# A macaron block on one Trainium2 core: the sums of exp(q) for every second chunk as pairwise additions on GpSimd, and new orders on all engines

## The reference

```python
x = x + 0.5 * ffn(layernorm(x))
x = x + attn(layernorm(x))
x = x + 0.5 * ffn(layernorm(x))

# ffn: lt = 16 tokens from token 1; m1, m2 are products of even and odd ones, per batch
h = gelu(x @ W1.T + scale * (x @ m1.T) + b1, exact)
out = h @ W2.T + scale * (h @ m2.T) + b2

# attn: 16 heads of 8, no softmax over keys
q, k, v = heads(x @ Wq.T + bq), heads(x @ Wk.T + bk), heads(x @ Wv.T + bv)
f(t) = exp(t/sqrt(8) @ R - 0.5 * sum((t/sqrt(8))**2))
kv = sum_n f(k)[n, :] v[n, :]
z = 1 / (sum_d f(q)[n, d] + 1e-8)
out = (z * (f(q) @ kv)) @ Wo.T + bo
```

## Time and profile before

| | us |
|---|---|
| median of 3 runs | 168.94 |
| the three runs | 169.96, 168.44, 168.94 |
| the profiled execution, own time | 168.41 |
| its span (first to last instruction) | 166.7 |
| busy: PE, DVE, ACT, POOL | 156.5, 125.6, 124.1, 91.3 |

### The profile page before, as it was taken

One profiled execution on the slowest core, in us unless ns is written; L12 is line 12 of the kernel. 1 busy time (PEld: TensorE's weight loads), 2 busy tenths in 40 slices (PEclk: granted clock), 3 DMA queues, 4 the chain that ended last, 5 costly groups with the idle time before them and its releaser, 6 DMA issues.

```text
span 166.7 us, 3400 instructions
## 1 busy us (share of the span) xinstructions
PE 156.5 (94%) x1036; PEld 139.1 (83%) x1036; DVE 125.6 (75%) x418; ACT 124.1 (74%) x249; POOL 91.3 (55%) x126
## 2 busy tenths in 40 slices
PE   6868999999999999899999998699999999999994
PEld 6835998999899889588898976588999989989993
DVE  1799895999489627999999999999997952582112
ACT  3399997687797999467999768899978564774330
POOL 5646648018999979968986892036513299000000
PEclk9999999999999999999999999999999999999999
DMA  4990445371213343322133124434346253255204
GB/s 101 325 292 16 128 129 189 127 193 64 64 65 110 83 148 107 122 67 65 42 110 104 67 65 126 159 95 130 139 117 203 91 152 97 95 152 167 63 0 126
DMA packets 31425, 19.55 MB, mean 117 GB/s; under 512 B 2624, under 2 KB 28464, under 8 KB 31408
## 3 DMA queue, kind: packets, MB, share of 16 engines
q1 hardware_dynamic: 30976, 19.27, 38.6%
q10 hardware_dynamic: 432, 0.07, 0.2%
HBM read 11.94 MB, written 7.40 MB: 116 GB/s over the span
## 4 chain that ended last, share of the span: by engine, by line
PE 83%; ACT 6%; DVE 4%; DMA 2%; issue 2%; SPq 1%; DVEq 0%; ACTq 0%
PE quad L811 33%; PE quad L792 9%; PE quad L793 8%; PE quad L794 8%; PE ps_g L846 4%; PE quad L828 4%; PE ps_t L865 4%; PE quad L830 3%; PE quad L829 3%; DMA X<-in_x_dram 2%; ACT xn L488 2%; PE ps_r L835 2%; ACT gl L528 1%; DVE ex L713 1%; ACT xn L493 1%
## 5 line engine op out<-in xcount | busy, mean ns | idle before, releaser
L811 PEld LDWEIGHTS quad<-w2e,gl 128*128 128x128 f32 x496 | 60.3, 192 | 2.7
L811 PE MATMUL quad<-w2e,gl 128*128 128x128 f32 x496 | 60.6, 275 | 0.0
L528 ACT ACTIVATE gl<-quad,cols 128x512 f32<-128x512 f32 x64 | 42.9, 685 | 15.2 <-PE quad L794 14.9
L792 PE MATMUL quad<-xh,w1h 128*128 128x512 f32 x64 | 28.6, 447 | 2.2 <-DVE xl L631 1.5
L488 ACT ACTIVATE xn<-X,nmr,rstd 128x128 f32<-128x128 f32 x61 | 25.1, 487 | 2.4 <-DVE nmr L603 2.4
L793 PE MATMUL quad<-xl,w1h 128*128 128x512 f32 x64 | 25.3, 395 | 0.0
L794 PE MATMUL quad<-xh,w1l 128*128 128x512 f32 x64 | 25.2, 394 | 0.0
L699 DVE TENSOR_TENSOR X<-quad,X 128x512 f32<-128x512 f32 (+1 forms) x16 | 10.6, 671 | 17.2 <-PE quad L811 16.0
L440 POOL TENSOR_TENSOR X<-X,b2h 128x512 f32<-128x512 f32 x16 | 21.5, 1368 | 0.2 <-DVE X L732 0.2
L413 POOL TENSOR_SCALAR veps<-mv 128x4 f32<-128x4 f32 (+1 forms) x16 | 4.8, 302 | 26.4 <-DVE mv L131 26.4
L415 POOL TENSOR_TENSOR rstd<-veps,mhalf 128x4 f32<-128x4 f32 (+1 forms) x16 | 16.4, 1027 | 1.3
(11 more groups left out here) (109 smaller groups left out, 280.7 us busy)
## 6 DMA issues: line engine op xcount, KB each, us to landing
ev<-token_rows SPq DMA_DIRECT2D x7, 512.0 KB, 3.8
folded<-tq SPq DMA_DIRECT2D x12, 256.0 KB, 2.0
land<-folded SPq DMA_DIRECT2D x48, 64.0 KB, 2.0
folded<-atq SPq DMA_DIRECT2D x8, 256.0 KB, 2.0
aland<-folded SPq DMA_DIRECT2D x32, 64.0 KB, 2.0
X<-in_x_dram SPq DMA_DIRECT2D x7, 256.0 KB, 6.5
out_dram<-X SPq DMA_DIRECT2D x7, 256.0 KB, 2.7
w1t<-in_w1t_dram SPq DMA_DIRECT2D x1, 256.0 KB, 3.5
```

Of the source, the lines that this page charges most:

```text
L528: act.activation(gl[:, f % 2, j], ps_h[j % 2], ACT.Gelu, bias=cols[:, j:j + 1]).then_inc(s_gelu, 1)
L792: pe.matmul(ps_h[j % 2], w1h[:, w, blk], xh[:, f % XT], start=True, stop=False)
L811: ins = pe.matmul(y[:, n * P:(n + 1) * P], gl[:, f % 2, j, n * P:(n + 1) * P], w2e[:, f // PER_B % 2, j], start=(j == 0), stop=(j == HB - 1))
```

## The change

For chunks 1, 3, 5 and 7 (`BY_PAIRS`) the stage `z_sums` is now GpSimd's: three additions, of the first and last four exponents of each head (256 results per partition), of the pairs of these (128), and of the last two (64), each behind the one before. The intermediate results lie in `wb`. The two waits on k_war and k_wv stand before the first. VectorE keeps chunks 0, 2, 4 and 6. All engines have a new order. Of the orders the diff below keeps the lines that the text speaks of.

```diff
+BY_PAIRS = (1, 3, 5, 7)
...
     "sp": (
...
-        "rows.4 put.9 put.10 land.9 land.10 rows.5 put.11 put.12 land.11 land.12 rows.6 put.13 down.8.3 put.14 "
...
+        "aland.1 aland.2 aput.4 aput.5 aland.3 aland.4 aland.5 aput.6 aland.6 aput.7 aland.7 put.8 land.8 rows.4 "
+        "rows.5 put.9 put.10 land.9 land.10 put.11 put.12 land.11 land.12 rows.6 put.13 put.14 land.13 land.14 "
...
     "pool": (
-        "stats.0 rest.0 stats.1 stats.2 stats.3 stats.4 stats.5 stats.6 stats.7 bias.0 bias.1 bias.2 astats.0 bias.3 "
-        "astats.1 bias.4 bias.5 bias.6 astats.2 abias.0 abias.1 astats.3 abias.2 abias.3 aturn.0 astats.4 astats.5 "
-        "aturn.1 bias.7 abias.4 abias.5 abias.6 aturn.2 astats.6 z_eps.0 aturn.3 z.0 z_eps.1 astats.7 aturn.4 z.1 "
-        "z_eps.2 abias.7 z.2 bias.8 aturn.5 stats.8 z_eps.3 z.3 aturn.6 stats.9 z_eps.4 bias.9 z.4 z_eps.5 aturn.7 "
-        "stats.10 z.5 stats.11 z_eps.6 stats.12 z.6 z_eps.7 z.7 stats.13 stats.14 stats.15 bias.10 bias.11 bias.12 "
...
+        "stats.0 rest.0 stats.1 stats.2 bias.0 bias.1 stats.3 stats.4 stats.5 stats.6 stats.7 abias.0 bias.2 bias.3 "
+        "astats.0 astats.1 bias.4 bias.5 aturn.0 astats.2 abias.1 abias.2 astats.3 astats.4 astats.5 bias.6 bias.7 "
+        "abias.3 aturn.1 astats.6 abias.4 abias.5 aturn.2 aturn.3 z_eps.0 abias.6 z.0 z_sums.1 z_eps.1 astats.7 "
+        "aturn.4 z.1 aturn.5 z_eps.2 stats.8 z.2 z_sums.3 aturn.6 z_eps.3 stats.9 z.3 aturn.7 z_eps.4 stats.10 "
+        "z_sums.5 z_eps.5 z.4 z.5 bias.8 bias.9 stats.11 z_eps.6 z_sums.7 stats.12 z_eps.7 z.6 stats.13 z.7 bias.10 "
+        "abias.7 stats.14 stats.15 bias.11 bias.12 bias.13 bias.14 bias.15 "
...
     "act": (
-        "norm.0 rest.0 first_w1h.0 first_w1h.1 first_w1h.2 turn.0 norm.1 load.0 first_w1h.3 up.0.0 turn.1 up.0.1 "
-        "norm.2 up.0.2 up.0.3 turn.2 norm.3 up.1.0 up.1.1 norm.4 up.1.2 up.1.3 w1h.1 norm.5 norm.6 up.2.0 turn.3 "
...
-        "anorm.6 feat.3.1 qturn.0 mix.0.1 anorm.7 exp.3.0 exp.3.1 aturn.5 feat.4.0 qturn.1 feat.4.1 gram.3 qturn.2 "
...
-        "turn.8 exp.6.0 gram.5 feat.7.0 norm.9 mix.2.1 qturn.4 norm.10 feat.7.1 w1h.4 exp.6.1 qturn.5 exp.7.0 exp.7.1 "
...
+        "norm.0 rest.0 first_w1h.0 first_w1h.1 turn.0 norm.1 first_w1h.2 first_w1h.3 up.0.0 turn.1 up.0.1 load.0 "
+        "up.0.2 up.0.3 norm.2 up.1.0 up.1.1 turn.2 norm.3 up.1.2 up.1.3 norm.4 norm.5 w1h.1 turn.3 norm.6 up.2.0 "
...
+        "norm.9 turn.8 norm.10 gram.5 feat.7.0 feat.7.1 qturn.3 exp.6.0 exp.6.1 w1h.4 mix.2.1 qturn.4 qturn.5 exp.7.0 "
+        "exp.7.1 up.8.0 up.8.1 turn.9 gram.7 up.8.2 up.8.3 up.9.0 up.9.1 turn.10 norm.11 up.9.2 up.9.3 norm.12 "
...
     "dve": (
...
-        "stats.2 first_w1l.0 norm.1 first_w1l.1 moments.2 turn.0 first_w1.3 stats.3 stats.4 norm.2 first_w1l.2 "
-        "stats.5 first_w1l.3 moments.3 moments.4 turn.1 stats.6 w2.0 norm.3 norm.4 moments.5 odd.1 turn.2 moments.6 "
...
-        "down.6.3 head_sums.0.0 ablocks.4 feat.0.0 astats.6 down.7.3 ablocks.5 amoments.6 astats.7 head_sums.0.1 "
-        "feat.0.1 head_sums.1.0 feat.1.0 z_sums.0 amoments.7 head_sums.1.1 feat.1.1 z.0 head_sums.2.0 z_sums.1 "
-        "feat.2.0 head_sums.2.1 feat.2.1 z.1 mix.0.0 z_sums.2 head_sums.3.0 feat.3.0 ablocks.6 head_sums.3.1 z.2 "
...
-        "z_sums.5 stats.10 head_sums.6.0 moments.10 feat.6.0 head_sums.6.1 o.3 feat.6.1 norm.9 turn.8 mix.2.0 "
-        "head_sums.7.0 odd.4 z.5 norm.10 feat.7.0 blocks.9 w1.4 blocks.10 stats.11 head_sums.7.1 w1l.4 feat.7.1 "
-        "moments.11 o.4 z_sums.6 stats.12 w2.4 turn.9 norm.11 moments.12 o.5 z.6 z_sums.7 stats.13 odd.5 mix.3.0 "
...
+        "stats.2 first_w1l.0 norm.1 moments.2 turn.0 first_w1.3 stats.3 first_w1l.1 norm.2 b2h.0 first_w1l.2 "
+        "first_w1l.3 moments.3 stats.4 turn.1 w2.0 moments.4 stats.5 stats.6 moments.5 moments.6 norm.3 stats.7 "
...
+        "down.6.3 astats.6 ablocks.4 ablocks.5 amoments.6 head_sums.0.0 feat.0.0 down.7.3 astats.7 head_sums.0.1 "
+        "feat.0.1 head_sums.1.0 feat.1.0 amoments.7 z_sums.0 head_sums.1.1 feat.1.1 z.0 head_sums.2.0 feat.2.0 "
+        "ablocks.6 head_sums.2.1 feat.2.1 z.1 head_sums.3.0 mix.0.0 feat.3.0 z_sums.2 head_sums.3.1 feat.3.1 o.0 "
...
+        "head_sums.6.0 head_sums.6.1 feat.6.0 z.4 norm.10 feat.6.1 odd.4 turn.8 blocks.9 blocks.10 head_sums.7.0 "
+        "mix.2.0 w1.4 z.5 head_sums.7.1 o.3 w1l.4 feat.7.0 feat.7.1 o.4 stats.11 z_sums.6 moments.11 stats.12 o.5 "
+        "turn.9 moments.12 norm.11 mix.3.0 z.6 w2.4 stats.13 odd.5 norm.12 moments.13 blocks.11 w1.5 blocks.12 z.7 "
...
     "pe": (
-        "lead.0 select.0 select.1 turn.0 up.0.0 turn.1 up.0.1 up.0.2 up.0.3 turn.2 up.1.0 up.1.1 down.0.0 down.0.1 "
-        "down.0.2 up.1.2 up.1.3 turn.3 down.0.3 down.1.0 down.1.1 down.1.2 up.2.0 up.2.1 split_weights.0 up.2.2 "
...
-        "mix.1.1 qturn.3 qk.6.0 o.2 qk.6.1 qk.6.2 qk.6.3 gram.5 o.3 qk.7.0 qk.7.1 mix.2.0 mix.2.1 qturn.4 qk.7.2 "
-        "qk.7.3 o.4 qturn.5 gram.6 up.8.0 up.8.1 o.5 gram.7 up.8.2 up.8.3 mix.3.0 up.9.0 up.9.1 down.8.0 down.8.1 "
...
+        "lead.0 select.0 turn.0 select.1 up.0.0 turn.1 up.0.1 up.0.2 up.0.3 up.1.0 up.1.1 down.0.0 turn.2 up.1.2 "
+        "down.0.1 up.1.3 down.0.2 down.0.3 down.1.0 down.1.1 turn.3 down.1.2 split_weights.0 up.2.0 up.2.1 down.1.3 "
...
+        "mix.1.1 o.2 qk.6.0 qk.6.1 qk.6.2 qk.6.3 gram.4 gram.5 qk.7.0 qk.7.1 qk.7.2 qk.7.3 mix.2.0 qturn.3 mix.2.1 "
+        "o.3 qturn.4 gram.6 qturn.5 o.4 up.8.0 up.8.1 o.5 gram.7 up.8.2 up.8.3 mix.3.0 up.9.0 up.9.1 mix.3.1 up.9.2 "
...
@@ -198,6 +198,9 @@
         vd = sb("vd", [P, 3])
         vs = sb("vs", [P, 3])
         wb = sb("wb", [P, 3, D])
+
+        z4 = wb[:, 0:2].rearrange("p k (m h d) -> p (k m) h d", m=2, h=HEADS)
+        z2 = wb[:, 2].rearrange("p (n h d) -> p n h d", n=NT, h=HEADS)
         wv2 = sb("wv2", [P, D])
         wah = sb("wah", [P, TOK], F32R)
         wal = sb("wal", [P, TOK], F32R)
@@ -264,6 +267,7 @@
             sem(f"s_{n}") for n in ("zs", "ze", "zr", "qn", "qt", "qte", "g", "o", "x2")]
 
         m_gs, m_kv, m_kvm, m_mp, m_mo = [sem(f"m_{n}") for n in ("gs", "kv", "kvm", "mp", "mo")]
+        s_pairs = sem("s_pairs")
         s_out = sem("s_out")
 
         folded = nc.dram_tensor("folded", (FC + CHUNKS, P, TOK), F32, kind="Internal").ap()
@@ -448,6 +452,20 @@
                     pool.wait_ge(a_hi, i + 1)
                     pool.tensor_tensor(as_tiles(xal[:, i % AH]), in_order(aland[:, i % ALAND]),
                                        as_tiles(xah[:, i % AH].bitcast(F32)), ALU.subtract).then_inc(a_lo, 1)
+                if stage == "z sums":
+                    mine = heads(qk[:, i % 2, :, 0, :])
+                    k = 2 * BY_PAIRS.index(i)
+                    pool.wait_ge(s_exp, 2 * i + 2)
+                    wait(pool, s_ze, i)
+                    if k == 0:
+                        pool.wait_ge(k_war, 1)
+                        pool.wait_ge(k_wv, 1)
+                    pool.tensor_tensor(z4, mine[:, :, :, 0:4], mine[:, :, :, 4:8], ALU.add).then_inc(s_pairs, 1)
+                    pool.wait_ge(s_pairs, k + 1)
+                    pool.tensor_tensor(z2, z4[:, :, :, 0:2], z4[:, :, :, 2:4], ALU.add).then_inc(s_pairs, 1)
+                    pool.wait_ge(s_pairs, k + 2)
+                    pool.tensor_tensor(zs[:, 0].rearrange("p (n h) -> p n h", n=NT), z2[:, :, :, 0], z2[:, :, :, 1],
+                                       ALU.add).then_inc(s_zs, 1)
                 if stage == "z eps":
                     pool.wait_ge(s_zs, i + 1)
                     wait(pool, s_zr, i)
```

## The result

The changed kernel takes 167.22 us (median of 4 runs, 166.9 to 167.42) against 169.43 for the kernel before (4 runs, 168.44 to 169.96): ratio 0.989, 95% interval 0.985 to 0.993. A later comparison gave 166.63 (6 runs) against 169.34 (10 runs), 0.982 with 0.978 to 0.987. So it is 1 to 2% faster. The kernel before scatters more than the changed one (168.28 to 170.71 over its 10 runs of the later comparison, against 166.25 to 167.1), and its profiled execution, 168.41, is one of its faster ones. Executions in a slower state of the chip are left out of every median here. The profiled execution of the changed kernel took 167.42 for a span of 165.7, 1.0 less than before, of 2.75 us forecast.

What follows compares the result with a forecast made beforehand. VectorE's queue was taken to set when up.8.0 starts, with TensorE dense behind it. Terms 2.25 + 0.8 - 0.3 = 2.75 us saved gave a median of 166.2; own range 164.9 to 167.6, with A and B 164.9 to 168.7.

Steps and rivals of the forecast that it cites:

- The attention stage, 2.25: VectorE's queue up to up.8.0 gets shorter: 2.55 - 0.5 + 0.2 = 2.25 us gained, ends 0 and 3.7.
- the 2.55: Work leaving VectorE's queue ahead of up.8.0: three z sums (1.77) and stats.11 (0.78), 2.55 us less.
- 0.5 for VectorE idle at its o.3 near 102: VectorE reaches o.3 at 101.7, TensorE's o.3 is done at 102.2, so VectorE stands idle for 0.5 us.
- The 1.77: Three of four z reductions taken off VectorE stand ahead of up.8.0, at 0.59 each: 1.77 us.
- The z chain, 1.6: GpSimd's three additions per odd chunk take 0.65, 0.43, 0.33 and waits, 1.6 us; the longer latency is covered.
- The start, 0.8: In the first 17 us, putting ScalarE's w2t scaling and norm.2 behind gelus gains 0.8 us, ends -0.3 and 1.2.
- The clash, 0.3: GpSimd's new additions exclude VectorE instructions with two SBUF inputs near w1.4 and w1l.4: 0.3 us lost.
- Behind up.8.0, nothing: TensorE stays full from up.8.0 to the end, so a microsecond saved before it is saved at the end.
- A (gaps only move): New order's kvm, qt and o.3 in a row eat the attention gain of 2.25: 168.4 us, chance 0.17.
- B: Rival: each of four pair chains on GpSimd holds up a VectorE instruction on the path, 2 us: 167.9, chance 0.1.
- C: Rival: TensorE's o.3 comes late behind qturn.3 and the slower z, ending at 107.9: 170.7 us, chance 0.08.
- D: Rival: all gaps closed, 3.7 in the attention stage plus 0.8 at the start: 164.4 us, chance 0.03.

Runs made afterwards that it cites:

- the one-word edit: The changed kernel with VectorE's feat.6.0 moved ahead of head_sums.6.1: 166.43 us, ratio 0.985 to the kernel before.
- the one sum of chunk 3: The changed kernel with chunk 3's z sum back on VectorE, behind head_sums.4.1: 167.17 us, ratio 0.991 to the kernel before.
- the queue cleared: Old orders, four sums on GpSimd, with bias.8 and bias.9 ahead of z.5 and abias.7 behind z_eps.6: 171.37 us, ratio 1.011 to the kernel before.
- the sums alone: The kernel before, in its old orders, with the z sums of chunks 1, 3, 5, 7 on GpSimd: 172.16 us, ratio 1.021.
- the one with the biases: Old orders, four sums on GpSimd, with abias.7, bias.8 and bias.9 moved behind z.5: 174.87 us, ratio 1.035 to the kernel before.

## Why the prediction was right or wrong

**The whole.** Forecast 166.2 with 164.9 to 168.7; measured 167.22 in the first comparison and 166.63 in the second. Direction and range held. Against the median before of the same comparison the gain is 2.2 and 2.7, of 2.75 forecast; the profiled span gained 1.0 and 1.7. That the 2.7 comes so near is in part luck: the forecast was made from one of the faster executions before, and the medians before lie 1.0 above it. By the lowest times the gain is 1.5 and 2.0. The parts held less well than the sum.

**The attention stage, 2.25: 1.67 and 1.73.** The stage did get shorter by what left VectorE's list, but this step is too large by 0.55, and what fills the 2.55 up again is not what I named. I put 0.5 for VectorE idle at its o.3 near 102; it did not wait:

```profile
104.32 0.68 DVE L750 TENSOR_TENSOR X<-ps_t,X 128x512 f32<-128x512 f32 x1
104.91 0.68 DVE L692 TENSOR_TENSOR w1l<-w1r,w1h 128x512 fp32r<-128x512 f32 x1
```

It came to o.3 at 104.32, not at 101.7, and TensorE's mix.2.0 at 101.52, not 99.7. (0.3 of each difference is the later first `up`.) The lateness began upstream, in TensorE's gaps: o.2 behind mo (0.8), then qk.7.0 behind feat.6.0 (0.5), the second of which the one-word edit shows (0.35 of the stage). I had added VectorE's queue as a sum of starts without its own waits and put only one new wait against it, 0.5; the changed kernel has two others, 0.51 and 0.45, for ScalarE. I had also put the wait of 1.4 down to VectorE, since "the exp itself comes behind VectorE's subtraction"; it was ScalarE's list that kept that exp for 5.3 us. up.8.0 was forecast at 105.8 less the start's gain and came at 106.69 and 106.09, short of the 107.5 that would have refuted it. Another sign of being wrong did come, a small one: TensorE's o.3 waits for qt (ScalarE is done with it at 102.98, o.3 starts at 103.07).

**What the sums do and what the orders do.** I forecast them as one. The runs part them: -0.59 and +2.74 alone, -1.67 together. The 1.77 that I booked for the sums is 0.6 in the stage (0.3 for the one sum of chunk 3), and the orders, for which my terms leave 0.78 - 0.5 + 0.2 = 0.5, are worth 1.1 where od doesn't meet qn (0.59 + 0.5). So the reason that I gave first carries a third of the gain. "Cover, then, until GpSimd runs over 2 us late" holds with the new orders, where VectorE's z never waits. With the old ones VectorE waited for z (1.33, and still 0.86 with the queue cleared) and TensorE for xal, which I had not priced at all.

**The z chain, 1.6: 1.57.** Its terms were 0.65, 0.43, 0.33 and are 0.73, 0.40, 0.29. That its length is hidden was right as well, with the new orders: with one addition in place of three B1 was 0.05 shorter.

**The start, 0.8: nothing.** At down.0.0 the forecast holds: it starts at 16.37 for 17.19 of the earlier trace rows, and first up to down.0.0 took 5.64 for 6.78, 1.1 less, of which 0.44 is turn.2:

```profile
14.89 0.47 PE L810 MATMUL quad<-xh,w1h 128*128 128x512 f32 x1 [0.16 <-ACT gl L546]
...
16.37 1.05 PE L829 MATMUL quad<-w2e,gl 128*128 128x128 f32 x8
```

But up.3.0 starts at 29.98 for 29.86, waiting for a gelu, which is only 0.2 ahead of before when counted from the first `up`, and A is 57.40 for 57.39. The step that failed is "a microsecond saved" at the start "is one saved at the end": ScalarE has the deferred load and norms still to do, and TensorE meets it again. With the start of before, A is 0.33 longer (57.73), above all nine with the new start, so the new start gives at least 0.3 and the rest of the new order of the first FFN takes it back.

**The clash, 0.3: none on the path here.** I took the additions for the danger and wrote that the moved biases cover the rest. Both halves were wrong. In the changed kernel GpSimd pays, being second:

```profile
99.67 1.52 POOL L477 TENSOR_TENSOR qn<-qk,zr 128x512 f32<-128x512 f32 x1
...
104.97 3.01 POOL L444 TENSOR_TENSOR X<-X,b2h 128x512 f32<-128x512 f32 x2
```

(1.08 and 2.55 undisturbed.) qn stands beside the xl of 99.57, the biases beside the w1l of 104.91, and nobody waits for either. The biases would be the costly ones: two of them on w1.4 cost 0.7 of the stage, and the three on all four of its instructions 2.5 (B2 of 11.78 for 9.29). "A clash costs 0.5" was read from one row; a single one cost 0.9 to 1.1 here (od 1.07 for 0.16, one w1 1.35 for 0.34, nmr 1.25 for 0.15), nearly the whole GpSimd instruction, whatever the size of VectorE's own.

**Behind up.8.0, nothing: +0.33 and +0.20.** C is longer by that. One gap of 0.25 is seen, ahead of up.9.0 (the last product before it starts at 111.35, it at 111.83). TensorE was not quite full from up.8.0 on, where I had it full. GpSimd's chain of chunk 7 took longer there (1.00 for its first addition at 111.26, beside w2.4), with nobody waiting. The rest of the 0.33 is not settled.

**The rivals.** A (gaps only move) is part of the truth: 0.5 of the stage and the start. B is real as a mechanism and not on the path in the changed kernel. C did not come: TensorE's o.3 ended at 104.2, 3.7 ahead of its point. D is out; some 2 us of gaps remain.

## What to carry to other kernels

Work moved to a less loaded engine is paid for in that engine's queue: before pricing its length, ask what stands behind it and who waits for that, and move the reorder with it. Look for small VectorE instructions with two inputs in SBUF that start within a long GpSimd addition, since each can cost nearly that whole addition; a word's place in the list can be worth more than the work's size. Work taken off a full engine gives back only what its next wait leaves: before booking it, look for the input that the engine will now be too early for. A lead won at the start counts only once it is still there at the stage that bounds the kernel; compare stretches between landmarks, not spans.

## What the runs showed of the hardware

A VectorE instruction of 8 columns took 1.07 and 1.08 where it takes 0.16, and one of 4 columns 1.25 for 0.15, each started 0.02 to 0.06 behind a GpSimd product or addition of 1.08, 1.09 or 1.29 us. Behind one of 0.73 the one of 4 columns took 0.69. In these runs the price follows the other engine's instruction.

TensorE's granted clock fell in two kernels, each time behind waits. With the sums alone it is 0.66 in 110:115, after 3.55 us of work in the 5 us ahead (rows above), and in the one with the biases 0.66 too, after 1.75:

```profile
105.00:110.00 5.00, 1.75 (x14) 1.36 (x12) 5.00 (x6) 2.44 (x7) 4.16 (x4) 1.00 0.14 52
110.00:115.00 5.00, 4.14 (x15) 3.53 (x16) 5.00 (x19) 4.01 (x7) 1.63 (x3) 0.66 0.50 144
```

0.66 is a mean: part of the stretch at 2.4 GHz, part at 1.2. In the cleared kernel it stays at 1.00 in that stretch. So a stall on the path can be paid twice: from up.8.0 to up.8.3 it took 5.53 with the sums alone and 5.01 with the biases, where it is 3.95 in the kernel before. On one row, gram's eight products took 1.71, for 1.06 in the changed kernel:

```profile
110.86 1.71 PE L868 MATMUL ps_g<-qk,xa 128*128 128x128 f32 x8 [4.10 <-ACT qk L564]
```
